# A decoder layer on one core: each engine's order of work in the attention layer rewritten over seven stages, and V copied in one instruction

## What is computed

```python
h1  = layernorm(x + hgrn_mixer(x))                     # ternary weights, quantized activations
q   = rope(h1 @ Wq)                                    # 32 heads of 8
k,v = split(ctx @ Wkv);  k = rope(k)                   # ctx: 128 rows x 128 per batch
h2  = layernorm(h1 + softmax(q k^T * 8**-0.5) v @ Wout + bout)
out = layernorm(h2 + quantized_gated_ffn(h2))          # 256 -> 1024 -> 256, silu gate
```

## Time and profile before

| | us |
|---|---|
| median of 3 runs | 418.39 (417.89 to 422.68) |
| the profiled execution, its own time | 418.04 |
| its span, first to last instruction | 416.3 |
| busy in the span: PE, DVE, ACT, POOL | 291.5, 288.5, 243.7, 219.5 |

### The profile page before, as it was taken

How to read it: one execution, slowest core, us unless ns; L and a number is a source line. 1 busy time by engine, 2 the same in 40 slices (tenths; PEclk the granted TensorE clock), 3 DMA queues, 4 the chain that set the end, 5 groups by cost and what they waited for, 6 DMA issues and landing times.

```text
span 416.3 us, 9865 instructions
## 1 busy us (share of the span) xinstructions
PE 291.5 (70%) x3140; PEld 183.2 (44%) x3140; DVE 288.5 (69%) x643; ACT 243.7 (59%) x533; POOL 219.5 (53%) x531
## 2 busy tenths in 40 slices
PE   0361654587762656899888888888877776998872
PEld 0131533365651433544555455455444432655541
DVE  4845889978973254535777777777776338899982
ACT  4257551547652320535676666666756455799994
POOL 4301437536877853525777666667711113467674
PEclk9976585879997865556999999999999578899998
DMA  7980000000001122114233333222240000011111
GB/s 199 334 274 2 0 2 0 1 0 0 2 1 28 31 57 59 21 40 59 59 61 59 61 60 60 58 58 58 51 53 4 1 2 0 0 41 38 38 34 55
DMA packets 48819, 20.38 MB, mean 49 GB/s; under 512 B 38033, under 2 KB 47889, under 8 KB 48785
## 3 DMA queue, kind: packets, MB, share of 16 engines
q1 hardware_dynamic: 48784, 19.95, 20.6%
HBM read 9.32 MB, written 2.10 MB: 27 GB/s over the span
## 4 chain that ended last, share of the span: by engine, by line
PE 32%; DVE 16%; issue 10%; POOL 7%; ACT 5%; DVEq 1%; POOLq 0%; SPq 0%; ACTq 0%
PE psum L906 7%; DVE M L816 5%; PE psum L947 5%; PE psum L923 4%; PE psum L876 4%; PE psum L892 3%; PE psum L933 2%; ACT PO L778 2%; PE psum L1200 2%; PE psum L940 2%; DVE AT L828 2%; DVE rs L824 1%; DVE region_q L1175 1%; DVE habs L1184 1%; DVE X L1188 1%
## 5 line engine op out<-in xcount | busy, mean ns | idle before, releaser
L816 DVE TENSOR_REDUCE M<-psum 128x8 f32<-128x1024 f32 x64 | 78.0, 1219 | 35.5 <-PE psum L876 35.4
L763 ACT ACTIVATE PB<-psum,exp_scale 128x1024 f32<-128x1024 f32 x64 | 71.8, 1121 | 28.4 <-PE psum L892 27.5
L906 PE MATMUL psum<-PB,region_g 128*32 128x128 f32 x1024 | 46.1, 303 | 0.8 <-ACT PB L763 0.8
L1200 PE MATMUL psum<-FW,FXT 128*128 128x512 f16 x128 | 33.7, 411 | 7.3 <-DVE FXT L1180 5.1
L876 PE MATMUL psum<-kt,region_t 32*128 32x128 f16 x512 | 28.1, 234 | 14.2 <-DVE M L816 12.9
L876 PEld LDWEIGHTS psum<-kt,region_t 32*128 32x128 f16 x512 | 15.9, 99 | 37.0 <-DVE M L816 27.6
L906 PEld LDWEIGHTS psum<-PB,region_g 128*32 128x32 f32 x1024 | 26.5, 118 | 10.5 <-issue 4.6
L892 PE MATMUL psum<-region_t,kt 32*128 32x128 f16 x512 | 27.6, 231 | 1.3 <-ACT PB L763 0.8
L1143 ACT ACTIVATE region_q<-psum,gs 128x512 f32<-128x512 f32 x32 | 20.6, 685 | 5.4 <-PE psum L1200 5.4
L1175 DVE TENSOR_TENSOR region_q<-region_q,psum 128x512 f32<-128x512 f32 x32 | 20.8, 684 | 3.6 <-PE psum L1200 2.3
L1200 PEld LDWEIGHTS psum<-FW,FXT 128*128 128x128 f16 x128 | 12.0, 103 | 24.3 <-issue 9.5
(11 more groups left out here) (212 smaller groups left out, 819.6 us busy)
## 6 DMA issues: line engine op xcount, KB each, us to landing
X<-in_x_dram SPq DMA_DIRECT2D x4, 512.0 KB, 6.7
out_dram<-X SPq DMA_DIRECT2D x16, 128.0 KB, 1.7
region_k<-in_L_ffn_w_gate_dram SPq DMA_DIRECT2D x1, 1024.0 KB, 12.3
region_k<-in_L_ffn_w_up_dram SPq DMA_DIRECT2D x1, 1024.0 KB, 9.9
region_k<-in_L_ffn_w_down_dram SPq DMA_DIRECT2D x1, 1024.0 KB, 11.4
CS<-in_ctx_dram SPq DMA_DIRECT2D x16, 64.0 KB, 2.2
region_t<-MT SPq DMA_DIRECT2D x64, 2.0 KB
region_w<-in_L_attn_Wi_dram SPq DMA_DIRECT2D x1, 256.0 KB, 3.8
```

Of the source, the lines that this page charges most:

```text
L763: act.activation(PB[c % 2][:], ps_P, ACT.Exp, scale=exp_scale[:, 0:1]).then_inc(exp_done, 1)
L816: dve.tensor_reduce(M[:, j:j + 2, n:n + 4], ps_L, AX.X, ALU.max).then_inc(max_done, 1)
L906: ins = pe.matmul(ps_v[R * g:R * g + R, c], V[(ph - lag) % NB][:, h], PB[c % 2][:, g // 2, 2 * (g % 2) + e], start=(e == 0), stop=(e == 1) ...
L1200: ins = pe.matmul(psx[n], XT[:, c], w[c][:, half(n)], start=(c == 0), stop=(c == DC - 1))
```

## The change

The pipeline gets seven stages; each engine's work is cut into named pieces with a lag, and the step lists them in a new order. Logits chunks 0 to 2 come at lag 1 and chunk 3 at lag 2, the first exponential at lag 2 and the others at lag 3, the transposes of PO at the end of lag 3, the rest of the output at lag 4, mean and variance at lag 5, the normalization at lag 6. K's low half and its transposing move one step back.

```diff
+    def load_values(sp):
+        for a in range(2):
+            for k in range(4):
+                to = WkvS[:, D + HD * (16 * a + 4 * k):D + HD * (16 * a + 4 * k + 4)].rearrange("p (i d) -> p i d", d=HD)
+                source = Wkv[:, D + HD * 16 * a:D + HD * (16 * a + 16)].rearrange("p (i k d) -> p i k d", k=4, d=HD)
+                sp.dma_start(to, source[:, :, k]).then_inc(v_in, 16)
...
     def sync(sp):
...
+            keys(2)
+            shifts(3)
+            context(0)
+            queries(1)
...
     def gpsimd(pool):
...
+            keys_low(1)
+            means(5)
+            queries(0)
+            deviation(5)
+            queries_low(0)
+            keys(0)
...
     def scalar(act):
...
+                act.activation(pairs[:, :, 0:4:3, 0:HD], ps_kv[:, D:2 * D].rearrange("p (g e d) -> p g e d", e=2, d=HD),
+                               ACT.Copy).then_inc(V_done, 1)
...
+            context(0)
+            exp(3, 1)
+            variance(5)
+            exp(3, 2)
+            keys(0)
+            values(0)
+            heads(4)
+            exp(3, 3)
+            sums(3)
+            exp(2, 0)
...
     def vector(dve):
...
+            normal(6)
+            reciprocal(4)
+            rowmax(2, 3)
+            negate(2)
+            heads(4)
+            maxima(2)
+            queries(0)
+            rowmax(1, 0)
+            rowmax(1, 1)
+            residual(4)
+            keys(0)
+            rowmax(1, 2)
...
     def tensor(pe):
...
+            context(0)
+            logits(2, 3)
+            logitsT(3, 1)
+            keys_values(0)
+            values(3, 0)
+            logitsT(3, 2)
+            maxima(2)
+            heads(4)
+            logits(1, 0)
+            values(3, 1)
+            logitsT(3, 3)
+            values(3, 2)
+            logits(1, 1)
+            output(4)
+            values(3, 3)
+            logits(1, 2)
+            logitsT(2, 0)
+            sums(3)
...
-                steps=Pipeline(B, 6, NB, 2), ...
+                steps=Pipeline(B, 7, NB, 2), ...
```

```diff
-        LAST_EXP = A_ALL - BESIDE + 1
+        FEED = 4
+        LAST_EXP = A_ALL - FEED
...
                 for s in range(A_END, A_ALL):
+                    if s == LAST_EXP + 1:
+                        act.preload_act_table_set("silu_and_others")
                         act.wait_ge(attn["rq_done"], B)
+                    attn["steps"].at(att, s)
...
-                    attn["steps"].at(att, s, after_exp=gate_up if s == LAST_EXP else None)
+                    attn["steps"].at(att, s)
+                    f = s - (A_ALL - FEED)
+                    if f >= 0:
+                        ffn["steps"].at(feed, f)
```

More of the change, by code:

```diff
@@ L682, in sync, with step, context, shifts @@
     def sync(sp):
[L683 to L690, removed]
+        def step(ph, *ts):
+            def context(lag):
+                t = ts[lag]
+                if t is None:
+                    return
+                i = (ph - lag) % 2
+                wait(sp, cT_done, t - 1)
+                sp.dma_start(CS[i][:], ctx_in[t]).then_inc(c_in[i], 16)
+            def shifts(lag):
+                t = ts[lag]
+                if t is None:
+                    return
+                i = (ph - lag) % NB
+                sp.wait_ge(MT_done, t + 1)
                 for j in range(4):
@@ L723, in rotate, with step, queries, keys @@
             nc.gpsimd.tensor_tensor(r[:], a[:], b[:], ALU.add).then_inc(done, 1)
[L725 to L741, removed]
+        def step(ph, *ts):
+            def queries(lag):
+                t = ts[lag]
+                if t is None:
+                    return
+                wait(pool, q2_done, t)
+                rotate(QS[:, t, :], qcos, qsin, t, rqA, rqB, RQ, rq_prod, rq_done)
+            def keys(lag):
+                t = ts[lag]
+                if t is None:
+                    return
+                pool.wait_ge(K_done, t + 1)
+                wait(pool, k2_done, t)
+                rotate(KS[:], kcos, ksin, t, rkA, rkB, RK, rk_prod, rk_done)
+            def keys_low(lag):
+                t = ts[lag]
+                if t is None:
+                    return
+                ka = KA[(ph - lag) % 2]
+                pool.wait_ge(k1_done, t + 1)
@@ L934, in step, with heads @@
                 ins.then_inc(poT_done, 1)
-            logits(3)
-            if t4 is not None:
-                pe.wait_ge(AT_done, t4 + 1)
+            def heads(lag):
+                t = ts[lag]
+                if t is None:
+                    return
+                pe.wait_ge(AT_done, t + 1)
                 at = AT[:].rearrange("p h d -> p (h d)")
@@ L1346, in _ @@
                     attn["steps"].at(att, k)
+                for s in range(BESIDE, A_LOOP):
+                    pool.wait_ge(mixer["Q_done"], s // 2 + 1)
+                    attn["steps"].at(att, s)
                 pool.wait_ge(mixer["Q_done"], NG)
-                for s in range(BESIDE, A_LOOP):
-                    attn["steps"].at(att, s)
                 attn["steps"].loop(pool, att)
@@ L1353, in _ @@
                     attn["steps"].at(att, s)
-                    if s >= A_ALL - BESIDE:
-                        ffn["steps"].at(feed, s - (A_ALL - BESIDE))
-                for s in range(BESIDE, F_LOOP):
+                    if s >= A_ALL - FEED:
+                        ffn["steps"].at(feed, s - (A_ALL - FEED))
+                for s in range(FEED, F_LOOP):
                     ffn["steps"].at(feed, s)
```

371 lines of the change are left out of this document (213 added, 158 removed).

## The result

The changed kernel takes 388.53 us (median of four runs, 386.85 to 398.46), the kernel before on the same chip 418.31: ratio 0.928, interval 0.918 to 0.938. Run again beside the experiments it took 395.98 (391.15 to 399.62; ratio 0.944, 0.933 to 0.954) and 394.22 (385.61 to 399.53; 0.926, 0.921 to 0.932). Ratios and intervals compare the fast runs of each set alone, those within 1.5% of its fastest; by the medians the three are 0.929, 0.948 and 0.944. So the changed kernel scatters by 14 us over its 15 runs (a fifth of the first set, 392.38, is among them), and the kernel before by 9 over its 35 (413.64 to 422.73). The 15 follow the mean granted clock: 0.900 and 385.61 us at one end, 0.854 and 399.62 at the other; a straight line through them falls 2.8 us for each hundredth.

The account below looks back on a forecast made before the run. No engine was full; PE was nearest, losing 1.6 us a step to hand-offs. Terms +2.5 + 0.5 − 12.5 − 8.5 + 1.5 = −16.5 from 418.0 gave 401.5, as median 401.9 us; range 391 to 411.

Parts of the forecast that it names:

- The start: Up to the context of step 3: +2.5 us, from -1 to +6; then steps 3 to 5 at half clock: +0.5.
- steps 3 to 5: Attention steps after the mixer, clock up after the same 31 us: +0.5 against 36.5 measured, from -8 to +5.
- the walk: Timing from trace rows: each instruction starts at its engine's last issue or releaser's hand-off; 8.5 us a new step.
- the clock rises earlier: Rival: fewer gaps in steps 3 to 5 lift the clock 20 us earlier, saving 8 more; 391 to 394, chance 0.2.
- The steady step: Attention steps 6 to 14: 8.7 us each, ends 8.3 and 9.5; nine steps give -12.5 us.
- The 0.15: Added to each steady step because the walk of the old order was some 0.15 us a step too short.
- The bound of 9.0: Steady step if VectorE's casts QA and KA each lose 0.4 us to POOL's port lock: 9.0 us a step.
- The K loop: Rival: K's transposing lands behind Q's, 4.6 us in place of 3.3; 9.55 a step, +10, 412, chance 0.1.
- The end: Step 15's context to the last residual: 43 us in place of 51.5, -8.5, ends 38 and 48.
- Behind it: Feed-forward after the last residual: first gate and up products no longer run ahead of it, +1.5 us (0 to 2.6).
- The slower rival: Clock stays at half: 5.7 us more for each step from 6 on; five such steps give 430, chance 0.04.

Follow-up runs that it names:

- experiment 2: The changed kernel with one extra TensorE wait ahead of the mixer's last step, until the first exponential is done: 391.4 us, ratio 0.942.
- experiment 8: The changed kernel run again unchanged, for the scatter of its clock: 395.98 or 394.22 us in the two repeats; the profile with the late rise spans 397.9.
- experiment 9: The changed kernel run again unchanged, the second repeat, as the measure beside other variants: 394.22 us, ratio 0.926.
- experiment 10: The changed kernel with V in four copies as before and its weight columns loaded unpermuted: 391.84 us, ratio 0.932.
- experiment 11: The changed kernel with feed-forward scales of tiles 0 to 11 moved between AT and the residual of steps 18 and 19 on VectorE: 387.31 us.
- experiment 1: The kernel before with 20 small TensorE products directly behind the last mixer product: 418.59 us, ratio 1.003.
- experiment 7: The kernel before with 20 small products behind the mixer's last product and 16 and 14 in the holes of step 3: 419.55 us, ratio 1.010.
- experiment 3: The changed kernel with the second logits group directly behind the first on TensorE (the pair order): 423.44 us, ratio 1.019.
- experiment 5: The pair order of experiment 3 with 18 small TensorE products filling its idle hole in steps 3 to 15: 411.42 us, ratio 0.986.
- experiment 12: Experiment 11's kernel with K's cast ahead of the residual and small products in three TensorE holes at the mixer's end: 380.85 us, ratio 0.909.
- experiment 4: The changed kernel with K's cast moved behind the last maximum of VectorE's step: 426.58 us, ratio 1.025.

## Why the prediction was wrong

**The step that failed** is in "The start": steps 3 to 5 "with the clock up after the same 31 us", +0.5. It was −10.5 in the profile. I kept from the trace of before how long the clock stayed at half and moved it into a new order, as if it were fixed. It is not. Of the six profiles with the new order whole (experiments 2, 8 to 11 and the first) three rose at 163 to 171 us, three at 182 to 184, and none as late as the 194 of both the first profile of before and that of experiment 1. Experiment 7 prices it: the old steps at nearly full clock take 28.9, so some 7.6 us are clock, and 28.9 − 26.0 = 2.9 are order. At full clock the walk was good: three steps of 8.7 are 26.1. Why the clock rises at 163 in one execution and at 183 in another, and why never so late as before, stays open.

**How far the number was off** is partly luck. With the rise at 183, as in the profile of experiment 8, the term is −4.5 in place of −10.5, and that run's 399.6 us lies in the range of 391 to 411, as do ten of the 15 runs and the medians of both repeats. Its total, −18.4 us, comes near −16.5 also because the late K took 4 us of the steady steps back.

**The rival "the clock rises earlier"** names what happened, with a chance of 0.2 and a price of 8 us in these steps; the first profile's rise was 31 us earlier, those of experiments 8, 10 and 11 some 11. What spoke against it was given too much weight. PE busy 15.45 of 16 us at half clock says that slow products fill time, and not when the clock will rise: in that stretch the old order issued 153 matmuls, and the new one, at full clock, 251 in 14.81 us. The Trainium skill (TensorE: Matmul & The Clock Gate, "What's actually happening") has sustained activity lift the clock and idleness take it away. The windows of experiment 1, with 22.36 us busy of 24 at 0.50, speak against the first alone. With the second experiments 3 and 5 agree in direction: the filled hole kept the clock that the open one lost. That a wait of 1.3 us can be enough is this case's measurement and not the section's.

**The steady step** was right: 8.66 for 8.7, and the walk's variants too: 9.9 for the pair's 9.86, 10.0 for 9.89 and 0.15. The 0.15 that I added for the walk's error was not needed in the new order's undisturbed steps (8.53 for 8.50); the mean of 8.66 comes from single steps of 8.7 to 9.15, so its closeness to 8.7 is in part luck. The bound of 9.0, by which QA's cast would be held up beside POOL, is out: the cast took 0.43 us at 210.89, where POOL was at work from 210.61 to 211.35, as the earlier trace rows has it for KA's with POOL done. The normalization took 0.55 to 0.70 beside POOL.

**The K loop** as a lasting bound did not come, but as a single late transposing it did, in three of those six profiles and in experiment 12: 4.8 to 5.3 us from issue to use for the assumed 3.3. In the three the clock then fell. I had priced lateness in steps, not in clock.

**The start**: +1.0 for +2.5, and 1.4 to 3.2 in the other whole profiles. **The end**: −4.5 for −8.5. I had 2.6 us for the scales in front of the reciprocal; they made PE stand 4.56, and in the half clock that came back at 279 us the rest was lost. In the profile of experiment 9, with the same wait, this stretch took 41.6 us. **Behind it**: FU of tile 4 comes 13.2 us after the last residual, 12.6 before, so +0.6 for +1.5; the remaining −1.9 is clock, half in parts of 345 to 357 us before, full from 318 on after.

**The slower rival** named the right danger, a step whose clock falls, in the wrong kernel: it is what experiments 3 and 4 do.

## What to carry to other kernels

Price an order twice: its waits by a walk of the engines, and the clock that TensorE has in it. Look at TensorE's longest single wait in a step, not only at its busy share: at 83 to 84% busy, one wait of 1.3 us a step lost the clock in seven of twelve steps, and waits of up to 0.7 us kept it. A reordering that left such a wait lost everything here, and products without use in it won 12 us back. Do not carry a stretch of low clock from the old trace into the forecast as if it were fixed; give its end a range from the mixer's end on, and a chance to match.

## What was not expected of the hardware

More work was faster: 216 small matmuls more, 13.7 us less in twelve steps. The same program, with the same waits at the mixer's end but for one of 0.16 us, saw its clock rise at 163 or at 183 us. An idle wait of 1.32 us was followed by half clock in some steps and not in others. And K's transposing DMA, 3.3 us in the page of before, took 4.8 to 5.3 in one step of several runs, three times near 231 us and once at 205; why is open, and was not tried.
